# A decoder kernel's Hyena filter stage: one pair of vector operations moved into the second level of the inverse transform, six rotations moved behind the second gate

## The reference, cut to what matters

```
for n in range(ORDER):                      # ORDER = 2 gates
    v_fft = rfft(v, n=2 * L)                # L = 1024
    h_fft = rfft(h[n], n=2 * L)
    y = irfft(v_fft * h_fft)[..., :L]
    v = y * x[:, n]                         # gate n
out = v.transpose(0, 2, 1) @ w_out.T + b_out
```

## Time and profile before

| | |
|---|---|
| median of three runs | 682.93 us |
| profiled execution, its own time | 682.95 us |
| its span in the profile | 681.0 us |
| PE busy | 650.6 us (96%) |
| DVE busy | 611.0 us (90%) |
| ACT busy | 384.5 us (56%) |
| POOL busy | 365.1 us (54%) |

### The profile page before, as it was taken

One profiled execution on the slowest core, in us unless ns is written; L12 is line 12 of the kernel. 1 busy time (PEld: TensorE's weight loads), 2 busy tenths in 40 slices (PEclk: granted clock), 3 DMA queues, 4 the chain that ended last, 5 costly groups with the idle time before them and its releaser, 6 DMA issues. The chain is left out here.

```text
span 681.0 us, 12462 instructions
## 1 busy us (share of the span) xinstructions
PE 650.6 (96%) x4284; PEld 476.8 (70%) x4284; DVE 611.0 (90%) x1241; ACT 384.5 (56%) x761; POOL 365.1 (54%) x506
## 2 busy tenths in 40 slices
PE   9999999999999999999999999888999999999996
PEld 3588765788747887568887677556777775666664
DVE  4899887999999999999999979748999979999997
ACT  3742157131368503475222634569888886888885
POOL 0633424537235753258451381284577769788786
PEclk9999999999999999999999999999999999999999
DMA  8730055230453446443743057552222221010012
GB/s 310 204 63 1 0 125 105 81 62 7 66 107 69 93 155 62 93 93 63 200 100 87 1 185 98 213 174 80 64 80 79 79 79 33 1 34 32 32 63 94
DMA packets 52680, 60.73 MB, mean 89 GB/s; under 512 B 5416, under 2 KB 46376, under 8 KB 52362
## 3 DMA queue, kind: packets, MB, share of 16 engines
q1 hardware_dynamic: 43498, 40.28, 18.3%
q0 software_dynamic: 8256, 18.86, 16.7%
q10 hardware_dynamic: 864, 0.79, 0.4%
HBM read 33.72 MB, written 11.53 MB: 66 GB/s over the span
## 5 line engine op out<-in xcount | busy, mean ns | idle before, releaser
L747 ACT ACTIVATE yb<-banks 128x256 f32<-128x256 f32 x64 | 24.1, 385 | 137.5 <-PE banks L446 92.3
L437 PE MATMUL banks<-inv_m,spec_y 128*128 128x256 f32 x384 | 85.5, 379 | 0.0
L473 PE MATMUL banks<-xt_in,w_in 128*128 128x512 f32 x192 | 84.5, 594 | 0.2
L437 PEld LDWEIGHTS banks<-inv_m,spec_y 128*128 128x128 f32 x384 | 73.0, 190 | 9.9
L389 PE MATMUL banks<-z_cplx,fwd_m 128*128 128x256 f32 x240 | 71.9, 381 | 3.5 <-DVE prod L1172 3.2
L390 PE MATMUL banks<-z_cplx,fwd_m 128*128 128x256 f32 x240 | 71.4, 379 | 0.0
L473 PEld LDWEIGHTS banks<-xt_in,w_in 128*128 128x128 f32 x192 | 36.1, 190 | 43.0 <-issue 40.2
L389 PEld LDWEIGHTS banks<-z_cplx,fwd_m 128*128 128x128 f32 x240 | 44.9, 190 | 11.8 <-issue 5.2
L390 PEld LDWEIGHTS banks<-z_cplx,fwd_m 128*128 128x128 f32 x240 | 45.6, 190 | 6.2
L904 POOL TENSOR_TENSOR spec_y<-prod 128x256 f32<-128x256 f32 x35 | 25.4, 726 | 42.0 <-DVE prod L1172 41.2
L2203 DVE TENSOR_REDUCE peak<-ps_score 128x16 f32<-128x1024 f32 x32 | 38.9, 1215 | 8.7 <-PE ps_score L1668 8.7
(11 more groups left out here) (311 smaller groups left out, 1704.4 us busy)
## 6 DMA issues: line engine op xcount, KB each, us to landing
x_tok<-in_x SPq DMA_DIRECT2D x8, 512.0 KB, 4.3
x_tok<-in_b_out POOLq DMA_DIRECT2D x8, 512.0 KB, 13.9
inv_scratch<-inv_sum SPq DMA_DIRECT2D x16, 256.0 KB, 2.6
xa_t<-inv_scratch SPq DMA_DIRECT2D x16, 256.0 KB, 2.7
v_t<-left POOLq DMA_DIRECT2D x8, 511.5 KB, 5.2
x_t<-left POOLq DMA_DIRECT2D x8, 511.5 KB, 5.6
xt_in<-in_x_t SPq DMA_DIRECT2D x3, 1024.0 KB, 5.9
x_scratch<-x_tok SPq DMA_DIRECT2D x6, 512.0 KB, 4.1
```

What stands on the lines that cost most here:

```text
L437: last = mm(bank[:, odd * 2 * P:(odd + 1) * 2 * P], spec_y[:, j + odd, part * D + h * P:part * D + (h + 1) * P], inv_m[:, o:o + 2 * P], st ...
L473: last = mm(proj_pair(b, t)[:, c * 512:(c + 1) * 512], w_in[:, k, TILES[t] * P:(TILES[t] + 1) * P], xt_in[:, k, c * 512:(c + 1) * 512], st ...
```

## The change

In `level_two` the m pair no longer writes into the place of the real pair (`ef`) but into that of the first complex group (`y2`), and a function can be run ahead of it (`between`). `level_one` can run its real pair alone or all but it. With that, three things move on the DVE at each boundary: the real pair of `level_one(u + 2, 0)` stands between the four sums and the m pair of `level_two(u + 1, 0)`; its three complex pairs stay behind the quarters; and its rotations stand in the next sequence, behind `right_tap` and ahead of `level_two(u + 2, 0)`. The number of operations is the same. The other engines' lists are unchanged.

```diff
-            def level_one(u, h, at=None, rotated=False):
+            def level_one(u, h, at=None, rotated=False, real=True, complexes=True):
...
-                dve.wait_ge(i_evac, 4 * i + 1)
-                signal(tt(ef[:, 0, :], IB[I_0][:, 0:Q], yb[:, I_0, :], ALU.add))
-                tt(ef[:, 1, :], IB[I_0][:, 0:Q], yb[:, I_0, :], ALU.subtract).then_inc(first_level, 1)
+                if real:
+                    dve.wait_ge(i_evac, 4 * i + 1)
+                    signal(tt(ef[:, 0, :], IB[I_0][:, 0:Q], yb[:, I_0, :], ALU.add))
+                    tt(ef[:, 1, :], IB[I_0][:, 0:Q], yb[:, I_0, :], ALU.subtract).then_inc(first_level, 1)
+                if not complexes:
+                    return
...
-                signal(tt(ef[:, 0, :], tmp[:, 1, 0:Q], tmp[:, 1, Q:2 * Q], ALU.subtract))
-                signal(tt(ef[:, 1, :], tmp[:, 1, 0:Q], tmp[:, 1, Q:2 * Q], ALU.add))
+                if between is not None:
+                    between()
+                signal(tt(y2[:, 0:Q], tmp[:, 1, 0:Q], tmp[:, 1, Q:2 * Q], ALU.subtract))
+                signal(tt(y2[:, Q:2 * Q], tmp[:, 1, 0:Q], tmp[:, 1, Q:2 * Q], ALU.add))
...
                     if not last_one:
                         right_tap(b + 1, T_LEAD)
+                    dve.wait_ge(vec_seq, seq.now())
+                    rotations(in_prod)
                     level_two(u, 0, tmp=past_xq, at=in_prod, u_real=u)
...
-                    level_two(u + 1, 0, tmp=past_xq, at=in_prod, u_real=u + 2)
-                    level_one(u + 2, 0, in_prod)
-                    dve.wait_ge(vec_seq, seq.now())
-                    rotations(in_prod)
+                    level_two(u + 1, 0, tmp=past_xq, at=in_prod, u_real=u + 2,
+                              between=lambda: level_one(u + 2, 0, in_prod, complexes=False))
+                    level_one(u + 2, 0, in_prod, real=False)
                     dve.wait_ge(*convolved(b, T_X1 + 1))
```

More of the change, by code:

```diff
@@ L1214, in level_one, with level_two @@
                         rotations(at, (g,))
-            def level_two(u, h, gate=None, dst=None, tmp=prod, at=None, u_real=None):
+            def level_two(u, h, gate=None, dst=None, tmp=prod, at=None, u_real=None, between=None):
                 i = 2 * u + h
@@ L1242, in quarter @@
                     if a == 1:
-                        return stt(yq[:, 1, :], ef[:, 0, :], ROOT_HALF, tmp[:, 3, Q:2 * Q], ALU.mult, ALU.add)
+                        return stt(yq[:, 1, :], y2[:, 0:Q], ROOT_HALF, tmp[:, 3, Q:2 * Q], ALU.mult, ALU.add)
                     if a == 2:
                         return tt(yq[:, 2, :], tmp[:, 3, 0:Q], tmp[:, 0, Q:2 * Q], ALU.subtract)
-                    return stt(yq[:, 3, :], ef[:, 1, :], -ROOT_HALF, tmp[:, 2, Q:2 * Q], ALU.mult, ALU.add)
+                    return stt(yq[:, 3, :], y2[:, Q:2 * Q], -ROOT_HALF, tmp[:, 2, Q:2 * Q], ALU.mult, ALU.add)
                 def gate_quarter(a):
```

## The result

The changed kernel takes 684.29 us, median of 20 executions (682.89 to 687.03); the kernel before, timed between them, 683.12 us (20 executions, 681.98 to 683.74). The ratio is 1.0017 to 1.0036 (95%), middle 1.0027. So the change costs 1.2 us, against a forecast of 0.5, and the time lies 0.1 us over the top of the range. The kernel before is itself 0.2 us above the 682.93 us of its first three runs, from which the range was worked out.

The account below looks back on a forecast made before the run. PE is busiest (96%), but the DVE's chain to the second right tap was taken to bound the first two boundaries. Terms 0 - 0 + 0.26 + 0.26 + 0 = +0.52 us on 682.95 gave 683.5 us, range 682.4 to 684.2.

Parts of the forecast that it names:

- PE's waits at L446: PE's inverse waiting for the DVE's real pair, 1.01 and 1.11 us at two boundaries; claimed to go, lengthening waits around `turn`.
- The rotations' move: Six DVE operations moved behind the right tap; claimed the DVE neither loses nor wins anything behind that tap.
- The DVE's chain to the right tap sets the turn: First two boundaries: only the DVE's chain up to the second right tap counts; PE's `turn` starts 0.06 us behind it.
- The later gate met the sums: POOL's later gate still runs when the DVE's sums of half 1 want to start; 0.26 us late at each of two boundaries.
- the second length: Time between the two `turn` starts at the first two boundaries; claimed 89.8 us instead of 89.56.
- The gate was not stretched: Judges the rival that the meeting lengthens POOL's gate to 3.41 us; 1.32 us a boundary, 685.6 us; chance 0.07.
- "Cost 0" at the third boundary: Products of the last unit: PE's first wait grows, its second shrinks, so the DVE's 0.26 us delay costs nothing.
- whose work comes from ACT: Third boundary: the DVE's 2.06 us wait for POOL, with POOL's work coming from ACT, covers the DVE's 0.26 us delay.
- that rival: The third boundary counts too: 683.7 us; chance 0.06 together with a wait that stays.
- The wait moves from L446 to L464 and the gates ahead of it. Saved at this boundary: 0: First two boundaries: PE's wait for the real pair only shifts to the turn and the gates ahead; 0 us saved.

Follow-up runs that it names:

- e1: Changed kernel with the real pair put back behind the quarters, so only the rotations move; 682.29 us, -0.25 against the kernel before.
- e8: Changed kernel with the moved rotations left out at all three boundaries, so part of the computation is missing; 681.99 us, -1.03 against the kernel before.
- e2: Changed kernel with the rotations put back ahead of the second gate, so only the real pair moves; 684.43 us, +1.89 against the kernel before.
- e4: Changed kernel with half a projection computed twice on PE ahead of the turn at the first two boundaries; 685.44 us, +2.9 against the kernel before.
- e5: The changed kernel run again, nothing further altered; 684.58 us, +1.56 against the kernel before.
- e6: Changed kernel with the transposes of the turn's second quarter issued twice at the first two boundaries; 684.23 us, +1.21 against the kernel before.
- e11: Changed kernel with two matmul calls (two instructions each) added behind the first turn; 686.01 us, beside 682.53 for the kernel before.
- e12: Changed kernel with four matmul calls (two instructions each) added behind the first turn; 686.76 us, beside 682.53 for the kernel before.
- e3: Changed kernel with POOL's boundary gate halved (columns 512 to 1023 left out) at the three boundaries; 683.00 us, +0.46 against the kernel before.
- e9: Kernel before with two matmul calls (two instructions each) added behind the first turn; 684.7 us, beside 682.53 for the kernel before.
- e10: Kernel before with four matmul calls (two instructions each) added behind the first turn; 686.08 us, beside 682.53 for the kernel before.
- e13: Changed kernel with POOL's boundary gate halved and one DVE sum computed twice at the first two boundaries; 685.55 us, +2.89 against the kernel before.
- e14: Changed kernel with POOL's boundary gate halved and one DVE sum computed three times at the first two boundaries; 688.73 us, +6.07 against the kernel before.
- e15: Kernel before with one DVE sum computed twice at the first two boundaries; 684.91 us, +2.25 against the unaltered kernel before.
- e7: Changed kernel with one DVE sum ahead of the second gate computed twice at the first two boundaries; 685.5 us, +2.5 against the kernel before.

## Why the prediction was wrong

**Right.** PE's waits at L446 went and came back at `turn`. The rotations' move was free (e1). The DVE's chain to the right tap sets the turn (e8: 1.42 us out, 1.42 us sooner). The later gate met the sums for 0.27 us, and the second length came out at 89.80 us, as forecast. The gate was not stretched. Held to the gate's end the sums would have begun at 267.93; they ended 0.96 us behind 267.52, at 268.48, so with their 0.69 us they began 0.14 us ahead of that, the same 0.14 us as in the earlier trace rows. The Trainium skill, page "SBUF — State Buffer", section "SBUF: two separate sides", calls the port pair that the DVE and GpSimd share an exclusive lock: whoever starts first has it for its whole instruction, and the other blocks. The trace agrees in kind and differs by these 0.14 us.

**Wrong, first: "Cost 0" at the third boundary.** The step that failed is "whose work comes from ACT". POOL's small operations (L960 to L966) start behind an ACT copy, but they are then held by the DVE's own L1072 (the first L963 ends 0.90 us behind it in both kernels), so the cover for the DVE's delay was tied to the DVE. That is read from the traces; no run takes this POOL work away from the DVE's. The cost itself is measured: 0.33 us with the collision and 0.0 to 0.1 us without it (62.69 to 62.74 in the profiles of the changed kernel, e2, e4, e5, e6, e11 and e12; 62.39 to 62.46 in those of before, e1, e3, e9, e10, e13, e14 and e15; e7, where the DVE waited longer for L390, has 62.63). The row was in the text already: L963 at 1.48 us beside the DVE and 1.02 alone; I used it only to price a longer gate. With this term the sum is 682.95 + 0.87 = 683.8 us, inside the range; that rival had been given part of 0.06. Counted from the 683.12 us of the kernel before beside the changed one, it is 684.0.

**Wrong, second: a term that was missing.** "The wait moves from L446 to L464 and the gates ahead of it. Saved at this boundary: 0" took full clock for granted. The changed kernel is low in half of its executions (15 of 30, against 0 of 72 of before), and a fall at the turn costs 1.1 us. Low clocks raise the median by 684.29 - 683.93 = 0.36 us and the slowest executions by 3 us. The 0.87 us of collisions and these 0.36 us come to 1.23, beside the measured 1.17. How much of the 0.36 us comes from falls at the turns is not known: of the two profiled executions, both low, one fell at the first turn and at 471 us, the other (e5) at 469 us only.

**Shown and not shown.** Shown: the collision and its price (e1, e3); that more idle time at the turn lowers the clock there with no collision (e13 and e14 against e3: 10 of 10 low against 1 of 11). Not shown: that the gathering is what does it in the changed kernel, or that the length of the idle time is all there is to it. e3 gathers as much as the changed kernel and had 1 low execution of 11; e8, with 0.95 us at the turn, had 3 of 8; e15, whose waits lie 26 us apart as in before, had 5 of 11, and e1, with 1.16 us at the turn against e15's 1.21, had 0 of 11. That all behind the first turn merely lies later is not ruled out either: e15 lies 1.4 us later than before by its lengths, but e10 lies 3.2 us later and had 0 of 5. The Trainium skill, page "TensorE: Matmul & The Clock Gate", section "What's actually happening", says that the chip's view of the activity doesn't start anew with a kernel, which would let equal executions differ; no run here tests it.

No version beat the kernel before: e1 is its equal, and e8 leaves work out.

## What to carry to other kernels

Removing the largest engine's wait buys nothing while another engine sets its next stop; ask what sets that stop, and take work out of that chain (e8), not merely out of its order. Each operation moved ahead of a POOL operation moves that too: look at what it will then run beside, and if both read two SBUF tensors, price the overlap. Moved idle time adds up to the same and may still not cost the same: with waits of 1.0 and 0.9 us, 26 us apart, no execution was low here; with about as much gathered within 10 us half of them were, and with waits of 1.0 and 1.2 us, 26 us apart, 5 of 11. So look at the granted clock of many executions, not only at the sum of the waits.

## What the hardware showed that I had not expected

- The hindrance works both ways. A POOL operation of 128x4 took 0.19 us alone and 0.42 or 0.73 us beside the DVE's L1072. This POOL step of small operations ended 0.90 us behind the DVE's two-input work in both kernels, and so passed the DVE's delay on.
- Counted back from its recorded end by its usual length, a two-input DVE operation that waited for POOL began 0.14 us ahead of the recorded end of POOL's operation, for sums of 128x512 (0.96 us for 0.69) and rotations of 128x128 (0.55 for 0.28) alike.
- At the turns the clock fell where no single wait of PE was longer than 1.8 us, with 1.2 to 1.5 us of transposes between two of them, and it stayed at 1.2 GHz for 3 to 4 us, in e14 for over 6.
